# Attention loop of a two-layer transformer kernel: heads turned and closed once per four quads, table products re-spaced

## The reference, cut to what matters

```python
q, k, v = split_heads(h @ Wq + bq), split_heads(h @ Wk + bk), split_heads(h @ Wv + bv)   # 16 heads of 8
scores = einsum('bhqd,bhkd->bhqk', q, k) / scale
c2p = take_along_axis(einsum('bhqd,hpd->bhqp', q, pos_k), c2p_pos)
p2c = take_along_axis(einsum('bhkd,hpd->bhkp', k, pos_k), p2c_pos)
scores = scores + (c2p + swapaxes(p2c, -1, -2)) / scale
probs = softmax(scores)
context = einsum('bhqk,bhkd->bhqd', probs, v)
```

## Time and profile before

| | |
|---|---|
| median of 3 runs | 825.57 us (823.41 to 828.2) |
| the profiled execution | 822.4 us, its span 820.7 us |
| busy in the span | PE 594.8, DVE 543.5, ACT 428.4, POOL 221.6 us |
| mean granted clock of TensorE | 0.828 of full speed |
| pace of rounds in the attention loop | 5.12 us with a table product, 4.22 us without |

### The profile page before, as it was taken

The page is one execution under the profiler, slowest core; times in us unless marked ns, Lnnn a source line. Parts: engine busy times, 40 slices in busy tenths (PEclk is TensorE's granted clock), DMA queues, the critical chain, the costliest instruction groups (busy, mean ns, idle before and its releaser), DMA issues. The chain is left out here.

```text
span 820.7 us, 16701 instructions
## 1 busy us (share of the span) xinstructions
PE 594.8 (72%) x5268; PEld 426.0 (52%) x5268; DVE 543.5 (66%) x1919; ACT 428.4 (52%) x912; POOL 221.6 (27%) x267
## 2 busy tenths in 40 slices
PE   4578918607999999899989996060994592576680
PEld 3377914304565666567656765050994372255470
DVE  7612243726777778699889992881225889766887
ACT  2034514406787888588868883120552433365532
POOL 1743422000930192039000003437342200212000
PEclk9969967957999999899989997655897655799655
DMA  9569427989999979995974410096553000000001
GB/s 247 175 198 372 151 65 206 318 305 254 252 346 261 271 224 347 242 247 155 356 163 121 123 40 14 2 253 169 172 179 91 0 1 0 1 1 1 0 1 51
DMA packets 132133, 130.74 MB, mean 159 GB/s; under 512 B 29152, under 2 KB 109040, under 8 KB 131408
## 3 DMA queue, kind: packets, MB, share of 16 engines
q1 hardware_dynamic: 126208, 97.27, 43.5%
q0 software_dynamic: 3728, 31.36, 9.8%
q10 hardware_dynamic: 2112, 1.05, 0.5%
HBM read 73.38 MB, written 52.88 MB: 154 GB/s over the span
## 5 line engine op out<-in xcount | busy, mean ns | idle before, releaser
L1306 DVE CUSTOM_DVE_ANT_0 l0am_prob<-l0am_ps_s,l0am_bias 128x512 f32<-128x512 f32 x256 | 161.9, 687 | 64.3 <-PE l0am_ps_s L1383 37.5
L1222 ACT ACTIVATE l0am_prob<-l0am_prob,l0am_neg_top 128x512 f32<-128x512 f32 x256 | 172.2, 730 | 25.8 <-DVE l0am_neg_top L1306 25.8
L1395 PE MATMUL l0am_ps_t<-c_ident,l0am_prob 128*128 128x128 f32 x1024 | 139.9, 281 | 0.0
L1395 PEld LDWEIGHTS l0am_ps_t<-c_ident,l0am_prob 128*128 128x128 f32 x1024 | 115.5, 144 | 16.8 <-issue 15.9
L1383 PE MATMUL l0am_ps_s<-l0am_ks,l0am_qs 32*128 32x512 f32 x512 | 76.8, 671 | 35.9 <-DVE l0am_neg_top L1306 27.0
L1216 ACT COPY l0am_probT<-l0am_ps_t 128x512 f32<-128x512 f32 x128 | 69.2, 589 | 53.2 <-PE l0am_ps_t L1395 53.2
L1293 DVE COPY l0am_probT<-l0am_ps_t 128x512 f32<-128x512 f32 x128 | 82.0, 682 | 3.8 <-PE l0am_ps_t L1395 3.8
L690 DVE COPY l0f_xsT<-l0f_psT 128x128 f32<-128x128 f32 x46 | 13.4, 292 | 101.9 <-PE l0f_psT L774 101.9
L565 ACT ACTIVATE l0f_h<-l0f_psU,l0f_experts 128x128 f32<-128x128 f32 x184 | 52.6, 368 | 44.9 <-PE l0f_psU L784 44.9
L1408 PE MATMUL l0am_ps_c<-l0am_probT,l0am_v 128*9 128x128 f32 x2048 | 68.8, 276 | 0.9 <-issue 0.9
L1020 POOL TENSOR_TENSOR l0am_near<-l0am_rows_q,l0am_rows_k 128x352 f32<-128x352 f32 (+7 forms) x24 | 31.3, 1341 | 133.2 <-DMA l0am_rows_k<-position_k 133.2
(11 more groups left out here) (309 smaller groups left out, 1036.7 us busy)
## 6 DMA issues: line engine op xcount, KB each, us to landing
l0am_bias<-near_terms SPq DMA_DIRECT2D x128, 192.0 KB, 4.6
near_terms<-l0am_near POOLq DMA_DIRECT2D x3, 6144.0 KB, 19.7
l0f_mine<-l0f_experts SPq DMA_DIRECT2D x46, 256.0 KB, 3.1
l0am_rows_k<-position_k SPq DMA_DIRECT2D x16, 448.0 KB, 6.6
near_terms<-l0am_near POOLq DMA_DIRECT2D x2, 3072.0 KB, 11.6
position_q<-l0am_rows SPq DMA_DIRECT2D x20, 224.0 KB, 4.0
l0am_rows_q<-position_q SPq DMA_DIRECT2D x20, 224.0 KB, 4.9
position_k<-l0am_rows SPq DMA_DIRECT2D x20, 224.0 KB, 4.4
```

The source lines that it names most:

```text
L1222: nc.scalar.activation(prob[:, k, :], prob[:, k, :], ACT.Exp, bias=neg_top[:, k:k + 1], scale=-1.0)\
L1306: dve.tensor_tensor_reduce(out=prob[:, k, :], in0=ps_s[:, j, :], in1=bias[:, j, at:at + S], scale=-1.0, scalar=HUGE, op0=ALU.add, op1=ALU.min,
L1395: last = pe.transpose(ps_t[:, u % 2, i, :], prob[:, u % SLOTS_, i * P:(i + 1) * P], ident[:, :])
```

## The change

Heads: headT and rate hold four quads. ScalarE copies the heads of quad q into place q % 4. In rounds 6, 10, 14, ... 66 (`turns_heads`) TensorE turns four quads' heads, one 128x128 transpose each, into the whole bank ps_g, and VectorE closes all four with one reciprocal (128x16) and one product (128x128).

Products: `late_quad` leaves rounds 1 to 12 as they were (batch 2) and puts the twelve of batch 3 into rounds 14 to 28 without 17, 21 and 25. ScalarE's `copy_rows` for the product of round q moves from the end of its round q to round q+1: to its very start where round q+1 turns heads, and else behind the two copies and the first two exponentials. Before each product TensorE waits for the copy of the product before. SP stores the chunk one round later.

```diff
--- before.py
+++ after.py
@@ -968,8 +968,8 @@
         bias = sb("bias", [P, GROUP, BIAS_COLS])
         prob, neg_top = sb("prob", [P, SLOTS_, S]), sb("neg_top", [P, SLOTS_])
         probT = sb("probT", [P, 2, GROUP, T4, P])
-        headT = sb("headT", [P, P])
-        rate = sb("rate", [P, GROUP])
+        headT = sb("headT", [P, T4, P])
+        rate = sb("rate", [P, T4, GROUP])
 
         ps_s = ps("ps_s", [P, GROUP, S])
         ps_t = ps("ps_t", [P, 2, T4, P])
@@ -1007,7 +1007,16 @@
 
         def late_quad(cn):
 
-            return cn - EARLY + 1
+            n = cn - EARLY
+            if n < BATCH_CHUNKS:
+                return n + 1
+            turn_, k = divmod(n - BATCH_CHUNKS, GROUP - 1)
+            return BATCH_CHUNKS + 2 + GROUP * turn_ + k
+
+        def turns_heads(q):
+            return q >= T4 + 2 and q % T4 == 2
+
+        LATE = {late_quad(cn): cn for cn in range(EARLY, B * BATCH_CHUNKS)}
 
         def view(what, offset, *dims):
             t = what[:, :].tensor
@@ -1133,7 +1142,7 @@
                             sp.wait_ge(near_out, 16 * (len(NEAR_PIECES) + b))
                         load_bias(n, t)
                         for cn in range(EARLY, B * BATCH_CHUNKS):
-                            if n and late_quad(cn) == 4 * (n - 1) + t:
+                            if n and late_quad(cn) + 1 == 4 * (n - 1) + t:
                                 store_chunk(cn)
                         if g == 0 and b + 1 < B:
 
@@ -1224,26 +1233,27 @@
 
                 def copy_heads(q):
                     act.wait_ge(weighed, q + 1)
-                    if q:
-
-                        act.wait_ge(heads_turned, q)
-                    nc.scalar.copy(headT[:, :], ps_c[:, 0:P]).then_inc(headT_ready, 1)
+                    if q >= T4:
+
+                        act.wait_ge(heads_turned, q // T4)
+                    nc.scalar.copy(headT[:, q % T4, :], ps_c[:, 0:P]).then_inc(headT_ready, 1)
 
                 for q in range(QUADS + 3):
+                    if q - 1 in LATE and turns_heads(q):
+                        copy_rows(LATE[q - 1], ps_g[:, :])
                     if 1 <= q <= QUADS:
                         copy_turned(4 * (q - 1))
                         copy_turned(4 * (q - 1) + 1)
                     if q < QUADS:
                         exp(4 * q)
                         exp(4 * q + 1)
+                    if q - 1 in LATE and not turns_heads(q):
+                        copy_rows(LATE[q - 1], ps_g[:, :])
                     if 2 <= q < QUADS + 2:
                         copy_heads(q - 2)
                     if q < QUADS:
                         exp(4 * q + 2)
                         exp(4 * q + 3)
-                    cn = EARLY + q - 1
-                    if EARLY <= cn < B * BATCH_CHUNKS:
-                        copy_rows(cn, ps_g[:, :])
 
             @block.vector
             def _(dve):
@@ -1307,25 +1317,24 @@
                                              scalar=HUGE, op0=ALU.add, op1=ALU.min,
                                              accum_out=neg_top[:, k:k + 1]).then_inc(neg_ready, 1)
 
-                def close_heads(q):
-
-                    n, t = divmod(q, T4)
-                    by_head = ps_g[:, 0:P].rearrange("p (j k) -> p j k", j=GROUP)
-                    dve.wait_ge(heads_turned, q + 1)
-                    dve.reciprocal(rate[:, :], by_head[:, :, DH]).then_inc(rates_ready, 1)
-                    dve.wait_ge(rates_ready, q + 1)
-                    dve.tensor_tensor(heads_out[:, t, n, :].rearrange("p (j d) -> p j d", j=GROUP), by_head[:, :, 0:DH],
-                                      rate[:, :].unsqueeze(2).broadcast_to((P, GROUP, DH)), ALU.mult).then_inc(heads_ready, 1)
-
-                for q in range(QUADS + 4):
+                def close_heads(n):
+
+                    by_head = ps_g[:, :].rearrange("p (t j k) -> p t j k", t=T4, j=GROUP)
+                    dve.wait_ge(heads_turned, n + 1)
+                    dve.reciprocal(rate[:, :, :], by_head[:, :, :, DH]).then_inc(rates_ready, 1)
+                    dve.wait_ge(rates_ready, n + 1)
+                    dve.tensor_tensor(heads_out[:, :, n, :].rearrange("p t (j d) -> p t j d", j=GROUP), by_head[:, :, :, 0:DH],
+                                      rate[:, :, :].unsqueeze(3).broadcast_to((P, T4, GROUP, DH)), ALU.mult).then_inc(heads_ready, 1)
+
+                for q in range(QUADS + 3):
                     if 2 <= q < QUADS + 2:
                         copy_turned(4 * (q - 2) + 2)
                         copy_turned(4 * (q - 2) + 3)
                     if q < QUADS:
                         for j in range(GROUP):
                             add_terms(4 * q + j)
-                    if 3 <= q < QUADS + 3:
-                        close_heads(q - 3)
+                    if turns_heads(q):
+                        close_heads(q // T4 - 1)
 
             @block.tensor
             def _(pe):
@@ -1409,20 +1418,18 @@
                                              probT[:, q % 2, j, i, :], start=(i == 0), stop=(i == T4 - 1), tile_position=(0, 32 * j))
                     last.then_inc(weighed, 1)
 
-                def turn_heads(q):
-                    pe.wait_ge(headT_ready, q + 1)
-                    if q:
-                        pe.wait_ge(heads_ready, q)
-                    pe.transpose(ps_g[:, 0:P], headT[:, :], ident[:, :]).then_inc(heads_turned, 1)
+                def turn_heads(n):
+                    pe.wait_ge(headT_ready, T4 * n + T4)
+                    for t in range(T4):
+                        last = pe.transpose(ps_g[:, t * P:t * P + P], headT[:, t, :], ident[:, :])
+                    last.then_inc(heads_turned, 1)
 
                 for q in range(QUADS + 3):
                     if q < QUADS:
                         score(q)
-                    cn = EARLY + q - 2
-                    if 3 <= q:
-                        if EARLY <= cn < B * BATCH_CHUNKS:
-                            pe.wait_ge(rows_ready, cn + 1)
-                        turn_heads(q - 3)
+                    if turns_heads(q):
+                        pe.wait_ge(rows_ready, max(LATE[k] for k in LATE if k < q) + 1)
+                        turn_heads(q // T4 - 1)
                     if 1 <= q <= QUADS:
                         turn(4 * (q - 1))
                         turn(4 * (q - 1) + 1)
@@ -1431,14 +1438,11 @@
                     if 1 <= q <= QUADS:
                         turn(4 * (q - 1) + 2)
                         turn(4 * (q - 1) + 3)
-                    cn = EARLY + q - 1
-                    if EARLY <= cn < B * BATCH_CHUNKS:
-                        if cn == EARLY + 1:
-                            pe.wait_ge(rows_ready, cn)
-                        if 3 <= q:
-
-                            pe.wait_ge(heads_ready, q - 2)
-                        row_products(cn, ps_g[:, :])
+                    if q in LATE:
+                        if q >= T4 + 2:
+                            pe.wait_ge(heads_ready, (q - 2) // T4)
+                        pe.wait_ge(rows_ready, LATE[q])
+                        row_products(LATE[q], ps_g[:, :])
 
         clear_semaphores(nc, own_sems + aside.own_sems)
```

## The result

The changed kernel takes 829.79 us (median of 20 runs) against 824.36 us: 1.0067 of the kernel before, 95% interval 1.0048 to 1.0086. It is 5.4 us slower. The forecast was 828.0, in a range of 822 to 836; it stood for a loss of 2.4 us over the 825.57 that were known then. The profiled execution took 830.25 us with a span of 828.4 us, 7.8 us over the profiled one of before. The runs of the changed kernel spread over 824.8 to 837.9 us, so a single pair of executions may differ from the medians by the 2.4 us that lie between 7.8 and 5.4.

A forecast was written before the change was run, and what follows sets the result against it. TensorE was taken to bound the attention loop. Product costs mostly paid by round 28's vanished stall, then +2.6 from the last stall, -0.7 from 18 rounds behind it, +0.5 closing: +2.4 on 825.57 gives 828.0 us, range 822.0 to 836.0.

The forecast's parts named there:

- The bound, the pace of rounds, the moved copy: Attention loop: TensorE bounds; rounds 4.05, turning 4.58; TensorE waits 0.78 us for the copy, making product rounds 5.70.
- 5.12 - 0.17 (heads) - 0.05: Product round before adding the wait: old 5.12 us, less the head transpose 0.17 and its wait for ScalarE's copy 0.05.
- My own upper bound: Product round behind a product: net cost up to +0.8 us if the weight load is fully exposed.
- Heads in fours: Attention rounds: three lose 0.17 us each, the turning one gains 0.36; four take 16.73 against 16.88, so -0.15.
- Turning rounds with a product: Rounds 6, 10, 14, 18, 22, 26: 5.45 us, as the copy stands first there and holds nobody.
- The waits of rounds 2 and 3 vanish: Loop start: they vanish into round 4's wait for a load of keys not paced by rounds; start stays 206.46.
- I let 6.6 us go: Round 28: its stall behind the second store, 4.06 and 2.55 us, disappears because four product rounds cover the landing.
- The tightest load: Bias loaded in round 23: lands near 330, wanted at 330.7 us, under 1 us of margin.
- the cover of the store is too thin: Rival, chance 0.22: the stall at round 27 or 28 stays; +5 to +9 us, 834.
- The last store slips by a round: Rival, chance 0.15: round 41's bias load gets out ahead; stall a round later, 4 us shorter; 824.
- The clock: Rival, chance 0.06: TensorE's clock falls in every third of 17 waiting rounds; 15 us more, 843.
- Tail: Last closing at the loop's end: adds 0.5 us, from three more transposes 0.36 and wider closing 0.18.

The follow-up runs named there:

- copy last: Changed kernel with ScalarE's copy of the product's rows put back to the end of its own round: 843.71 against 846.59 us, 0.9985 of the kernel before.

## Why the prediction held, and where its sum was off

- *The bound, the pace of rounds, the moved copy*: right, and shown. The wait stands in 17 rounds, as counted; the edit that removes it takes back the loss. Its size was 5.81 - 5.12 = 0.69 us per round, and I had 0.58. The difference comes in about equal parts from two terms. Without the wait such a round lasts 4.97 (copy last), where "5.12 - 0.17 (heads) - 0.05" gives 4.90: with the head transpose gone, the turn behind it costs 0.06 more. And the wait costs 5.81 - 4.97 = 0.84 us, where I had 0.78. My own upper bound was 0.8 for the whole.
- *Heads in fours*: -0.15 per four rounds was wrong; the profile shows 0. Three rounds lose 0.11 each and the turning one gains 0.33.
- *Turning rounds with a product*: 5.45 forecast, 5.40 measured.
- *"The waits of rounds 2 and 3 vanish"*: not quite. Round 4 started at 207.24, 0.8 us late.
- *"I let 6.6 us go"* was the step that failed most. The forecast put the second store near 309.4, because SP would run 3 us ahead; it went out at 314.14, 1.8 us later than before. SP did not run ahead: it was through with the loads of rows for that batch at 281.4 us instead of 279.5, as it had begun them at 261.04 instead of 258.36. The tightest load was named rightly, the bias that is loaded in round 23: it took 19.4 us to land, 2.6 us too late for round 27. The rival "the cover of the store is too thin" came true by half: 3.3 us of the 6.6 stayed. That a bias load that is late also holds the copy, the product and the scores behind it was missing from my working.
- *The last store slips by a round*: no; it moved by 8.4 us (399.89 against 391.45), and the rounds with it (round 29 by 8.1 us, 338.60 to 346.68). The forecast had +2.6 for it.
- *The clock*: 1.00 from 207 to 330 us with TensorE idle 0.61 us in most rounds. This rival fell. What the Trainium skill (TensorE: Matmul & The Clock Gate, A second HAM failure mode: psum-queue depth-cycling) says of short recurring gaps did not happen in these rounds: the granted clock stayed at 1.00.
- *Tail*: from ScalarE's last copy of heads to the end of the loop are 1.65 us, where it was 1.09; the 0.5 us more that I gave are about right.

In all, the sign and the mechanism were right, and the size was too small: round costs too low, the hidden part too large. The profile shows how the sum missed. Round 29 was forecast at 340.9 and came at 346.68, 5.8 us later: 0.8 from the start of round 4, 1.7 from the pace of the rounds, 3.3 from the stall. So the forecast of +2.4 us stands against +5.4 in the medians and +7.8 in the profiled pair. That 828.0 lies only 1.8 us under the measured 829.79 is partly luck: the 825.57 it started from was 1.2 us above the median before of the 20 runs.

## What to carry to other kernels

When a copy out of a shared bank is moved, look for every later writer of that bank, and compare the copy's new end with the moment that writer is due; what stands ahead of the copy on its own engine counts, busy or waiting. Fewer, wider instructions gained nothing here, where the engine they relieve isn't the bound. A kernel that waits for loads behind a periodic large store can hide part of a slowing of its rounds, as it seems to have done here: take the store out of both versions once, and the cost of the rounds shows.

## What I had not expected of the hardware

Eight 128x128 fp32 transposes that follow one transpose take 0.97 us to the start of what comes next, and 1.03 directly behind the four scores; the lone transpose between took 0.16, where one in a row of eight takes 0.12. So in both orders some 0.05 us fall on the transpose that comes first behind the scores.

The same program, the changed kernel, took 829.8 us in the result and 853.95 on chip 4. Two profiles of it show where: round 1 began at 188.39 and at 197.75 us, from the scores of round 1 to those of round 63 passed 308.0 and 308.5 us, and 332.0 and 345.9 us followed. The attention loop, which TensorE bounds, took the same; the stages around it did not. Why was not tried.
